# Second graph's attention as three one-pass products of split parts, with a rewritten order in the first graphs

## The reference, cut to what matters

```python
# x: (16, 512, 256) float32, adj: (16, 512, 512) int32, 0 or 1; W_fc (32, 256), W_attn (1, 64)
h = x @ W_fc.T;  f1 = h @ a1;  f2 = h @ a2
scores = leaky_relu(f1[:, :, None] + f2[:, None, :], 0.2)
attn = softmax(where(adj == 0, -1e9, scores), axis=2)
x = layernorm(x + elu(attn @ x))
xn = x / sqrt(max(sum(x * x), 1e-12))
out = layernorm(x + ((xn @ xn.T) @ adj) @ x)
```

## Time and profile before

| what | value |
|---|---|
| time, median of 3 runs | 332.82 us (332.80 to 333.58) |
| the profiled execution | 332.77 us, its span 330.8 us |
| PE busy | 319.3 us (97%) |
| weight loads (PEld) busy | 299.7 us (91%) |
| DVE busy | 282.0 us (85%) |
| ACT busy | 291.0 us (88%) |
| POOL busy | 206.9 us (63%) |
| granted TensorE clock, mean | 0.997 |

### The profile page before, as it was taken

One profiled execution on the slowest core, in us unless ns is written; L12 is line 12 of the kernel. 1 busy time (PEld: TensorE's weight loads), 2 busy tenths in 40 slices (PEclk: granted clock), 3 DMA queues, 4 the chain that ended last, 5 costly groups with the idle time before them and its releaser, 6 DMA issues.

```text
span 330.8 us, 7276 instructions
## 1 busy us (share of the span) xinstructions
PE 319.3 (97%) x2376; PEld 299.7 (91%) x2376; DVE 282.0 (85%) x1000; ACT 291.0 (88%) x606; POOL 206.9 (63%) x236
## 2 busy tenths in 40 slices
PE   8999999999999999999999999999999999999992
PEld 5777999989999999999999999999999989998881
DVE  4899899788998989898998989898998988947635
ACT  4898799989999999999999999999999998984561
POOL 4036774956635595766668585766669576665623
PEclk9999999999999999999999999999999999999998
DMA  8665444414416346545535544643544641210121
GB/s 233 215 177 144 131 124 130 127 65 129 128 16 194 111 130 171 147 128 132 181 73 169 151 129 133 183 132 93 176 116 130 187 130 65 64 65 0 58 71 63
DMA packets 32965, 41.38 MB, mean 125 GB/s; under 512 B 1153, under 2 KB 24737, under 8 KB 32929
## 3 DMA queue, kind: packets, MB, share of 16 engines
q0 software_dynamic: 15888, 24.12, 27.0%
q1 hardware_dynamic: 16992, 16.81, 16.1%
q10 hardware_dynamic: 48, 0.00, 0.0%
HBM read 32.54 MB, written 8.39 MB: 124 GB/s over the span
## 4 chain that ended last, share of the span: by engine, by line
PE 82%; DVE 8%; POOL 4%; issue 3%; ACT 1%; POOLq 0%; DVEq 0%
PE ps_l L1283 14%; PE ps_l L1239 9%; PE ps_l L1240 9%; PE ps_h L1209 8%; PE ps_h L1210 7%; PE ps_h L1211 7%; PE ps_probT L1186 7%; PE ps_l L1269 4%; PE ps_l L1271 4%; PE ps_l L1270 4%; PE ps_l L1251 3%; DVE product L446 2%; PE ps_h L1206 2%; PE ps_f L1175 1%; POOL y L280 1%
## 5 line engine op out<-in xcount | busy, mean ns | idle before, releaser
L1209 PE MATMUL ps_h<-x_hi,probT_hi 128*128 128x256 f32 x224 | 68.3, 305 | 1.2 <-issue 0.7
L1239 PE MATMUL ps_l<-xn_hi,adj_sb 128*128 128x256 f32 x256 | 63.7, 287 | 0.9 <-DVE xn_lo L529 0.7
L1210 PE MATMUL ps_h<-x_lo,probT_hi 128*128 128x256 f32 x224 | 62.5, 279 | 0.0
L1283 PE MATMUL ps_l<-w_sb,xnT 128*128 128x256 f32 x256 | 62.3, 380 | 0.2
L1211 PE MATMUL ps_h<-x_hi,probT_lo 128*128 128x256 f32 x224 | 62.5, 279 | 0.0
L1240 PE MATMUL ps_l<-xn_lo,adj_sb 128*128 128x256 f32 x256 | 62.4, 283 | 0.0
L313 POOL TENSOR_TENSOR xn_lo<-xn,xn_hi 128x1024 fp32r<-128x1024 f32 x15 | 36.1, 2404 | 34.5 <-ACT xn_hi L876 34.5
L1239 PEld LDWEIGHTS ps_l<-xn_hi,adj_sb 128*128 128x128 f32 x256 | 48.9, 191 | 2.3 <-DVE xn_lo L529 1.1
L1283 PEld LDWEIGHTS ps_l<-w_sb,xnT 128*128 128x128 f32 x256 | 45.2, 190 | 5.9 <-issue 1.0
L1240 PEld LDWEIGHTS ps_l<-xn_lo,adj_sb 128*128 128x128 f32 x256 | 48.9, 191 | 0.0
L446 DVE CUSTOM_DVE_ANT_0 product<-x_sb,v_bcast 128x256 bf16<-128x256 f32 x128 | 47.0, 425 | 0.0
(11 more groups left out here) (82 smaller groups left out, 813.8 us busy)
## 6 DMA issues: line engine op xcount, KB each, us to landing
adj_sb<-adj POOLq DMA_DIRECT2D x15, 1024.0 KB, 5.9
x_sb<-x SPq DMA_DIRECT2D x16, 512.0 KB, 4.6
out<-o_sb SPq DMA_DIRECT2D x15, 512.0 KB, 3.2
x_hi<-x POOLq DMA_DIRECT2D x14, 512.0 KB, 4.1
adj_sb<-adj POOLq DMA_DIRECT2D x4, 256.0 KB, 4.6
out<-o_sb SPq DMA_DIRECT2D x4, 128.0 KB, 1.7
wfc<-w_fc SPq DMA_DIRECT2D x1, 32.0 KB, 1.9
attn_cols<-w_attn ACTq DMA_DIRECT2D x1, 0.2 KB, 1.7
```

The costliest lines, as they stand in the source:

```text
L1209: nc.tensor.matmul(ps, probT_hi[:, c, blk], x_hi[n][:, k, :], start=(k == 0), stop=False)
L1210: nc.tensor.matmul(ps, probT_hi[:, c, blk], x_lo[n][:, k, :], start=False, stop=False)
L1239: nc.tensor.matmul(ps, a, xn_hi[n][:, k, :], start=(k == 0), stop=False)
L1283: last = nc.tensor.matmul(ps, xnT[:, d, c * P:(c + 1) * P], w_sb[:, d, :], start=(d == 0), stop=(d == DC - 1))
```

## The change

`WHOLE_P` goes from 2 to 1. Graph 1's attention is thereby made of three one-pass products: 48 matmul instructions where there were 32. It needs x_hi of graph 1 (one more transfer of 512 KB on POOL's queue), `split_x(1)` on POOL, four `probT_hi_part(1, c)` on ACT, and four subtractions in place of copies in `probT_lo_part(1, c)`. The order in which the steps of graphs 0 to 4 stand on POOL, DVE, ACT and PE is written anew; the loop and what follows it are the same. The first lines of the difference, and three places of ACT's and PE's order:

```diff
-WHOLE_P = 2
+WHOLE_P = 1
...
+            load_x_hi(1)
             residual_sum_part(0)
             load_adj(2)
-            load_x_hi(3)
             residual_sum_part(1)
             residual_sum_part(2)
             residual_sum_part(3)
-            load_x_hi(2)
+            split_x(1)
             shifted_moments(0)
             power(0)
+            load_x_hi(2)
...
             lrelu(0, 0)
             lrelu(0, 1)
-            lrelu(0, 2)
             softmax_exp(0, 0)
             softmax_exp(0, 1)
+            lrelu(0, 2)
+            lrelu(0, 3)
             softmax_exp(0, 2)
-            lrelu(0, 3)
             softmax_exp(0, 3)
...
+            attend(0, 0)
             transpose_prob(0, 2)
-            attend(0, 0)
             transpose_prob(0, 3)
             attend(0, 1)
+            attend(0, 2)
             bcast_f2(1)
-            attend(0, 2)
             attend(0, 3)
             transpose_prob(1, 0)
             transpose_prob(1, 1)
-            attend(1, 0)
-            attend(1, 1)
             transpose_prob(1, 2)
             transpose_prob(1, 3)
             bcast_f2(2)
+            attend(1, 0)
+            attend(1, 1)
             attend(1, 2)
             attend(1, 3)
...
+            node_scores(4, 1)
             normalise(1)
...
```

More of the change, by code:

```diff
@@ L621, in _ @@
             probT_lo_part(0, 1)
+            denominators(0)
+            residual_part(0)
             probT_lo_part(0, 2)
-            denominators(0)
+            probT_lo_part(0, 3)
             node_scores(1, 1)
             node_scores(1, 0)
-            residual_part(0)
-            probT_lo_part(0, 3)
             masked_f2(1, 0)
+            residual_part(1)
+            residual_part(2)
             masked_f2(1, 1)
@@ L633, in _ @@
             node_scores(2, 1)
+            negate_max(1, 1)
+            residual_part(3)
+            row_moments_part(0)
             probT_lo_part(1, 0)
-            negate_max(1, 1)
-            residual_part(1)
-            residual_part(2)
             probT_lo_part(1, 1)
-            row_moments_part(0)
-            residual_part(3)
             row_moments_part(1)
-            denominators(1)
             row_moments_part(2)
             row_moments_part(3)
+            denominators(1)
+            node_scores(2, 0)
             probT_lo_part(1, 2)
-            node_scores(2, 0)
             probT_lo_part(1, 3)
+            masked_f2(2, 0)
             normalise_part(0)
@@ L948, in _ @@
             elu_relu(0, 1)
+            elu_exp(0, 2)
+            elu_relu(0, 2)
             lrelu(1, 0)
+            elu_exp(0, 3)
+            elu_relu(0, 3)
             lrelu(1, 1)
-            elu_exp(0, 2)
+            lrelu(1, 2)
             softmax_exp(1, 0)
             softmax_exp(1, 1)
-            elu_relu(0, 2)
-            lrelu(1, 2)
             lrelu(1, 3)
-            elu_exp(0, 3)
-            elu_relu(0, 3)
+            probT_hi_part(1, 0)
+            probT_hi_part(1, 1)
             softmax_exp(1, 2)
             softmax_exp(1, 3)
+            probT_hi_part(1, 2)
+            probT_hi_part(1, 3)
+            make_mask(2)
             elu_exp(1, 0)
@@ L969, in _ @@
             xn_hi_first(2)
+            elu_exp(1, 2)
+            xn_hi_first(3)
             elu_relu(1, 2)
-            xn_hi_first(3)
             elu_exp(1, 3)
@@ L1012, in _ @@
             elu_relu(2, 3)
-            lrelu(3, 3)
             copy_xnT(1, 0)
+            copy_xnT(1, 1)
             probT_hi_part(3, 0)
@@ L1018, in _ @@
             softmax_exp(3, 3)
+            copy_w(1, 0)
             make_mask(4)
+            copy_w(1, 1)
             probT_hi_part(3, 2)
             probT_hi_part(3, 3)
-            copy_w(1, 0)
-            copy_w(1, 1)
-            copy_xnT(1, 1)
+            lrelu(4, 0)
+            lrelu(4, 1)
             elu_exp(3, 0)
             elu_relu(3, 0)
+            elu_exp(3, 1)
+            xn_hi_part(2)
+            elu_relu(3, 1)
             normalise2(0)
-            xn_hi_part(2)
-            elu_exp(3, 1)
-            elu_relu(3, 1)
-            lrelu(4, 0)
-            softmax_exp(4, 0)
-            elu_exp(3, 2)
-            lrelu(4, 1)
-            lrelu(4, 2)
-            scale_z(2, 0)
-            elu_relu(3, 2)
-            elu_exp(3, 3)
+            elu_exp(3, 2)
+            elu_relu(3, 2)
+            lrelu(4, 2)
+            elu_exp(3, 3)
+            scale_z(2, 0)
+            softmax_exp(4, 0)
             softmax_exp(4, 1)
@@ L1088, in _ @@
             make_mask(6)
+            elu_relu(5, 0)
             xn_hi_part(4)
-            elu_relu(5, 0)
-            lrelu(6, 0)
             elu_exp(5, 1)
             elu_relu(5, 1)
+            lrelu(6, 0)
             elu_exp(5, 2)
@@ L1348, in _ @@
             make_out(1, 3)
+            attend(3, 2)
             attend(3, 3)
```

119 lines of the change are left out of this document (58 added, 61 removed).

## The result

| | before | after |
|---|---|---|
| time, median (lowest to highest) of 4 runs each, taken together | 333.1 us (332.8 to 333.58) | 336.63 us (335.66 to 336.84) |
| the profiled execution, its span | 332.77 us, 330.8 us | 336.79 us, 335.0 us |
| granted clock, mean | 0.997 | 0.988 |

The ratio is 1.0099, with a 95% interval of 1.0074 to 1.0124: slower by 1.0%, or 3.3 us (the two medians lie 3.5 us apart). The forecast was 335.1 us in a range of 333.3 to 337.0.

A forecast was written before the change was run, and what follows sets the result against it. DVE's queue was taken to bound the kernel until make_z(0, 0) at 33.10, PE afterwards. Terms 1.7 + 0.6 + 0.1 = 2.4 us, less perhaps 0.1 given back, on 332.8 gave 335.1 us, range 333.3 to 337.0.

The forecast's parts named there:

- the added step: DVE before xn_lo of graph 0: masked_f2(2, 0) now stands ahead of normalise_part(0), 0.6 us.
- Start (gain 0.5): Start of graph 0: first exp at about 10.2, DVE's first copy at 11.85 instead of 12.36, 0.5 us gained.
- The two holes on DVE: DVE in graph 0: waits of 1.2 us before the reciprocal and 0.95 us before the first exp_h.
- ACT, POOL, transfer: Other holders of make_z(0, 0): POOL covered by 0.5 us, ACT's copies done by 29.0, x_hi of graph 1 costs nothing.
- The clock: Rival: clock falls in PE's new hole, graph 1's products up to 5.6 us more, 338 to 341 us; chance 0.10.
- the forecast's own signs of being wrong: make_z(0, 0) before 34, granted clock under 1.00 between 21 and 35, or POOL or mask release before DVE's normalisation.
- Term 2: Behind make_z(0, 0): PE waits 0.6 us before make_w(0, 0), as lrelu and exp delay ACT's copies of z.
- term 3: At make_z(1, 0): DVE waits for POOL's sum, xn_lo of graph 1 comes at about 49.3; another 0.1 us.
- Given back: Later graphs: perhaps 0.1 us returned, up to 0.5, out of PE's 1.6 us of later waits.
- The likeliest case: Terms 1 to 3 delay make_z(0, 0) and what follows; 334.2 to 336.0 us by itself, chance 0.68.
- PE's saving lands: Rival: without DVE's holes make_z(0, 0) starts when PE is done, at 31.9, so 331.6 us; chance 0.08.

The follow-up runs named there:

- the run with both fillers: Changed kernel plus 24 keep-warm matmuls on PE after attend(0, 3) and 16 between transpose_prob(1, 1) and (1, 2); 334.44 us.
- the run with the second filler: Changed kernel plus only the 16 keep-warm matmuls between transpose_prob(1, 1) and (1, 2); 336.0 us.
- the old order with one-pass products: Kernel before with WHOLE_P = 1, the steps that form needs, and a few steps exchanged on DVE and ACT; 337.25 us.
- the last kernel: Kernel before up to make_z(1, 0), changed kernel's order beyond, float32 products in graph 1, node_scores(4, 1) moved ahead of normalise(1); 331.76 us.
- the first: Changed kernel plus only the 24 keep-warm matmuls between attend(0, 3) and transpose_prob(1, 0); 334.83 us.
- the run with z first: Changed kernel with keep-warm matmuls in both holes, and lrelu(2, c) and softmax_exp(2, 0) put back behind the copies of z on ACT; 334.82 us.

## Why the forecast was right or wrong

**Direction and range held, the range by luck**; the sum came out 1.5 us short, as errors of opposite sign stood in it. Up to `make_z(0, 0)` the forecast had 1.7 us and the profiled execution lost 4.57: 1.65 is the holes and the added step (34.75 - 33.10, from the run with both fillers, start gain included), 0.5 the start gain that was not had, 2.4 the fall of the clock. Against that the later graphs gave back 1.29 where 0.1 was forecast. Without this 336.63 would have been about 337.8 and outside the range.

**Start (gain 0.5).** Not had in the profiled execution: the first copy began at 12.42, not 11.85. PE's 28 keep-warm matmuls took 4.08 us, because the clock rose late in them (the trace's record of the full clock begins at 9.6 us of the span); in the kernel before they took 3.43 (8.3 us) and with both fillers 3.58 (8.6 us), where the copies began at 11.93. The reordering of lrelu and exp did what it should: the first exp started at 10.19, forecast 10.2. When the clock rises differs by execution, and the forecast took the 3.43 of one execution as fixed.

**The two holes on DVE.** Right: 1.16 and 1.03 with the clock at 1.00. In the changed kernel the first was smaller (0.66), as DVE came later to the same reciprocal, and the second larger (1.52).

**ACT, POOL, transfer.** Right with the clock up. POOL's powers ended at 31.91 and the normalisation started at 32.66, behind `masked_f2(2, 0)`; in the run with fillers it started at 31.95, against the forecast 31.9. `split_x(1)`, the four copies and x_hi delayed nothing there.

**The clock.** The step that failed: "Against it: transposes go on in between", and with it the chance of one in ten. The transposes did go on (eight between the holes of 2.97 and 1.62 us), and the clock was at 0.50 from 26.7 us on all the same; all four executions of the changed kernel have a mean clock of 0.986 to 0.988. It is one of the forecast's own signs of being wrong. The forecast had the holes right, 3.1 us and another of which it said only that the transposes came between waits, and read them as harmless because the one fall in the trace came behind a longer one. The rival's price was too high, 338 to 341 for the total; the fall costs 2.2 to 2.9 us, since it lay on the second transposes and on only sixteen of the 48 products, and ACT's queue adds 0.3. The Trainium skill's warning (TensorE: Matmul & The Clock Gate, Why this matters for your kernels) of idle gaps between bursts of matmuls is borne out by this trace. The length of one gap alone does not decide here: behind 2.97 us the clock fell in the changed kernel and not in the run with the second filler, and it fell behind 1.04 and 1.22 us in the old order with one-pass products.

**Term 2 and term 3.** `make_w(0, 0)` came 5.40 us after `make_z(0, 0)`, before 4.81: 0.59, forecast 0.6 (only 0.24 of it shows as a wait). From there to `make_z(1, 0)` 9.32 instead of 9.04: 0.28, forecast 0.1.

**Given back.** Forecast 0.1 and at most 0.5, measured 1.29. The term was read from PE's list of waits, 1.6 us in all. Most of the loss isn't in that list: in the two stretches above PE shows busy 25.12 of 25.33 and 19.13 of 19.31, 0.39 idle together, and yet the new order does the same work 0.89 + 0.47 = 1.36 sooner. A matmul row here is 0.28 us long where the next starts 0.12 later, so a pause shorter than the 0.16 of overhang counts as busy. Only the distance between starts showed it. Behind these two stretches the orders are equal again: from 91.59 to 320 us before, and from 95.69 to 324.10 in the changed kernel, both 228.41 us.

**What rivals came true.** The likeliest case and the clock's together. "PE's saving lands" did not, nor did it in the old order as tried: there the form and the moves that came with it cost 2.0 us.

## What to carry to other kernels

Judge a new order by the start-to-start distances of a step that every graph has, one stage at a time: here one stage lost 5.4 us and the others won 1.3, and the mixed kernel with the old first stage beats both. A hole on an engine is a cost twice when TensorE's clock can fall in it; price holes of a microsecond or more ahead of a burst of matmuls with part of the burst at half clock, and with what is queued behind its results. When work moves on VectorE or GpSimd, look at what then lies beside GpSimd's large elementwise operations.

## What the hardware showed that was not expected

**A VectorE product stands still beside GpSimd's 128x1024 subtraction.** Both its operands are in the on-chip buffer: 2.57 and 2.19 us instead of 0.42, three times in two of the tried kernels, each ending 0.3 us behind a subtraction of POOL. The kernel before has one too, in its last graphs, and so has every run (0.99 to 1.00 us, at 270 to 276 us). It could have been read before the forecast; VectorE's and GpSimd's row of the kernel before:

```profile
271.54 0.99 DVE L446 CUSTOM_DVE_ANT_0 product<-x_sb,v_bcast 128x256 bf16<-128x256 f32 x1
```
```profile
269.85 2.38 POOL L269 TENSOR_TENSOR x_lo<-x_sb,x_hi 128x1024 fp32r<-128x1024 f32 x1
```

Moving the subtraction (337.25 to 334.82 us) or the products (336.91 to 331.76) removes the long ones. The Trainium skill (SBUF — State Buffer, SBUF: two separate sides) has this as a lock on a shared port, which a VectorE operation with two SBUF inputs and a GpSimd operation that reads SBUF take from each other for the whole instruction; these rows agree. It would have the same for products beside `powers`, a GpSimd operation of 1.71 us on 128x8 elements, and there the trace does not agree: the product at 40.80 in the last kernel lies inside powers (40.05 to 41.76) and takes 0.43. Operations of VectorE that read their other operand from the matmul banks were not slowed beside x_lo: the probT_lo pair at 26.41 in the changed kernel took 1.29 while POOL's subtraction ran from 26.68 to 29.05.

**The clock does not rise or fall at the same point in every execution.** The same hole of 2.97 us was followed by a mean clock of 0.50 in the changed kernel and of 1.00 in the run with the second filler alone, whose executions lie between 334.15 and 337.21 us. What decides between them was not settled. The rise at the start matters as well, in these runs to the new order alone: where the clock did not fall, the first copy at 11.93, 12.34, 12.48 and 12.73 us gave `make_z(0, 0)` at 34.75, 35.19, 35.34 and 35.58 (both fillers, the second, the first, and the run with z first). In the old order the keep-warm matmuls took 3.43 to 4.11 us in three kernels with the old start, and make_z stayed at 33.1 to 33.2, since there the first transposes wait for ACT's exp until 11.66 us in any case (0.36 us in the kernel before).
